# The last recurrent steps of a fused network on one Trainium2 core: state products on a 128 by 128 block diagonal, and extra products in the gaps

## What is computed

```python
h = concat(mean_over_hidden(einsum(x, W) + b), txt)     # 64 x 96 x 64
h = h + ssm_4_layers(layernorm(h))                      # state space layers
h = h + moe_top2_of_16(layernorm(h))                    # two-layer experts
h = h + attention_8_heads(layernorm(h))                 # causal, strict
h = h + lstm(layernorm(h))                              # 96 steps, one after the other

def lstm_step(h, c, x_t):                               # U_*, V_*: 64 x 64
    i = sigmoid(x_t @ U_i + b_i + h @ V_i)
    g = tanh(x_t @ U_c + b_c + h @ V_c)
    o = sigmoid(x_t @ U_o + b_o + h @ V_o)
    c = h * c + i * g
    h = o * tanh(c)
    return h, c
```

## Time and profile before

| what | value |
|---|---|
| median of 3 runs | 833.98 us (831.4 to 834.63) |
| the profiled execution's own time | 833.69 us |
| its span, first to last instruction | 832.0 us |
| first matmul of step 32, the first exposed one | 700.61 us into the span |
| share of the span in which PE is busy | 83% |
| mean granted clock of TensorE | 0.854 of full speed |

### The profile page before, as it was taken

The page is one execution under the profiler, slowest core; times in us unless marked ns, Lnnn a source line. Parts: engine busy times, 40 slices in busy tenths (PEclk is TensorE's granted clock), DMA queues, the critical chain, the costliest instruction groups (busy, mean ns, idle before and its releaser), DMA issues.

```text
span 832.0 us, 16450 instructions
## 1 busy us (share of the span) xinstructions
PE 691.6 (83%) x6414; PEld 408.9 (49%) x6414; DVE 515.8 (62%) x1098; ACT 372.8 (45%) x694; POOL 228.9 (28%) x203
## 2 busy tenths in 40 slices
PE   3677788954579999988899899989899998887775
PEld 3675545633442222245234344347577776565553
DVE  3765675568956555366458766558777774345643
ACT  2232444431424455645444455545565654333332
POOL 4156754474600032111023210214422422000000
PEclk9989789776569999999999999999899999555555
DMA  9840000000035343200232222200000000000000
GB/s 186 144 81 10 1 1 1 2 0 1 0 98 176 106 130 123 72 2 3 88 102 78 63 90 87 52 1 2 2 2 2 2 2 4 8 11 7 11 9 12
DMA packets 42402, 36.85 MB, mean 44 GB/s; under 512 B 20888, under 2 KB 29848, under 8 KB 42328
## 3 DMA queue, kind: packets, MB, share of 16 engines
q1 hardware_dynamic: 41242, 35.57, 16.4%
q10 hardware_dynamic: 1088, 0.26, 0.2%
HBM read 33.85 MB, written 1.97 MB: 43 GB/s over the span
## 4 chain that ended last, share of the span: by engine, by line
PE 55%; DVE 25%; ACT 7%; issue 6%; POOL 3%; DMA 2%; SPq 1%; DVEq 0%; POOLq 0%; ACTq 0%
PE PS L1656 10%; PE PS L1643 10%; PE PS L1619 6%; PE PS L1691 3%; PE PS L1670 3%; DVE XC L991 3%; PE PS L1605 2%; PE PS L1747 2%; PE PS L1758 2%; PE PS L1712 2%; DVE st L973 2%; DMA BIG<-in_x 2%; ACT Y L700 2%; DVE st L989 2%; DVE am L1171 2%
## 5 line engine op out<-in xcount | busy, mean ns | idle before, releaser
L1656 PE MATMUL PS<-Y,W1f 64*128 64x512 f32 x384 | 110.5, 653 | 4.8 <-DVE Y L1132 2.5
L1643 PE MATMUL PS<-XC,w2s 128*64 128x512 f32 x384 | 105.2, 627 | 0.4 <-ACT BIG L736 0.4
L1619 PE MATMUL PS<-LS,V 64*64 64x32 f32 x1140 | 70.6, 270 | 29.2 <-DVE LS L1274 29.0
L745 ACT ACTIVATE XC<-PS 128x1024 f32<-128x1024 f32 x68 | 69.3, 1021 | 53.6 <-PE PS L1643 44.9
L1619 PEld LDWEIGHTS PS<-LS,V 64*64 64x64 f32 x1140 | 58.6, 187 | 69.5 <-DVE LS L1274 66.2
L1132 DVE TENSOR_TENSOR Y<-XD,UF 128x512 f32<-128x512 f32 x96 | 67.6, 715 | 14.4 <-DMA UF<-gd 8.8
L604 POOL TENSOR_TENSOR st<-st,mhalf 128x8 f32<-128x8 f32 x12 | 21.5, 1795 | 186.5 <-DVE st L1119 186.5
L1261 DVE SCALAR_TENSOR_TENSOR LS<-LS 128x32 f32<-128x32 f32 x96 | 19.5, 203 | 63.5 <-ACT LS L860 39.9
L1643 PEld LDWEIGHTS PS<-XC,w2s 128*64 128x64 f32 x384 | 19.3, 136 | 74.2 <-issue 65.3
L1656 PEld LDWEIGHTS PS<-Y,W1f 64*128 64x128 f32 x384 | 29.9, 187 | 50.0 <-issue 25.5
L178 POOL TENSOR_TENSOR st<-st,mhalf 128x8 f32<-128x8 f32 x24 | 39.3, 1637 | 37.6 <-DVE st L976 37.6
(11 more groups left out here) (239 smaller groups left out, 1434.7 us busy)
## 6 DMA issues: line engine op xcount, KB each, us to landing
UF<-gd SPq DMA_DIRECT2D x192, 128.0 KB, 2.9
BIG<-in_x SPq DMA_DIRECT2D x8, 512.0 KB, 12.2
out<-X SPq DMA_DIRECT2D x48, 32.0 KB, 2.0
W1f<-in_L_ffn_w SPq DMA_DIRECT2D x2, 512.0 KB, 6.3
EX<-in_L_ffn_w SPq DMA_DIRECT2D x1, 1024.0 KB, 16.3
H<-in_txt SPq DMA_DIRECT2D x2, 256.0 KB, 12.5
w2s<-in_L_ffn_w SPq DMA_DIRECT2D x1, 512.0 KB, 9.2
gd<-EX SPq DMA_DIRECT2D x6, 64.0 KB, 1.7
```

Of the source, the lines that this page charges most:

```text
L745: act.activation(Hb[:, b:b + 2, :], PS[:, b:b + 2, :], ACT.Relu).then_inc(S("m_h"), 1)
L1619: mm = pe.matmul(PS[r, b, o:o + HN], V3[r, g, :], HB[r, (t - 1) % 4, :], start=False, stop=True, skip_group_check=True)
L1643: mm = pe.matmul(PS[64 * h:64 * h + 64, 6, :], w2s[:, 2 * p + h, :], Hb[:, n % 2 * 2 + h, :], start=(p == 0), stop=(p == E // 2 - 1))
L1656: mm = pe.matmul(PS[:, n % 2 * 2 + h, :], W1f[r, 2 * p + h, :], Rb[r, n % 4, :], start=True, stop=True)
```

## The change

1. A tile `VB` holds the three state matrices twice, on the diagonal of a 128 by 128 block each, with zeros elsewhere. GpSimd fills it (one memset, two copies) between the scaling of V and the subtraction on `W1f`. In the exposed steps `gates_h` makes one product per gate with weights of 128 by 128 for both halves of the batch, where there were two with 64 by 64. Steps 0 to 31 keep the pairs.
2. In every exposed step but the last, and but those with `last_project`, `att_out` or `turn_x`, PE makes one more product at the end of the slot, of `W1f` with n columns of `w2s`, whose result is read by nothing (banks 0 or 1 of PSUM, free at that time). n is 256, 448, 176 or 272 by t % 4, and 160 more in the slots where chunk 4 or 5 is normalised.
3. `last_project` moves to t = 33, 35, 37 and 39, and chunk 4 begins at t = 45 in place of 49.
4. The 24 transposes of `att_out` and `turn_x` of chunks 4 and 5 become matmuls with the identity.

```diff
+        VB = sb("VB", [128, 3, 128])
...
-        XB = (3 * E + 2, 3 * E + 13, None, None, NPR + 18, NPR + 34)
+        XB = (3 * E + 2, 3 * E + 13, None, None, NPR + 14, NPR + 34)
...
-        LAST_O = [XS + 1 + 4 * c for c in range(NP)]
+        LAST_O = [XS + 1 + 2 * c for c in range(NP)]
...
+            seq(pool.memset(VB[:, :, :], 0.0), "VB")
+            for h in range(2):
+                r = slice(64 * h, 64 * h + 64)
+                seq(pool.tensor_copy(VB[r, :, r], V3[r, :, :]), "VB")
...
+            def turn_block(c, k, src):
+
+                dst = PS[:, x_bank(c), k * 128:(k + 1) * 128]
+                if x_bank(c) == 0:
+                    return pe.matmul(dst, src, ident[:, :], start=True, stop=True)
+                return pe.transpose(dst, src, ident[:, :])
...
                     else:
+
                         b, o = (2 + gate_pair(k), (2 * s + g) * HN) if g < 2 else (6 + gate_pair(k), s * HN)
-                    for h in range(2):
+                        mm = pe.matmul(PS[:, b, o:o + HN], VB[:, g, :], HB[:, (t - 1) % 4, :], start=False, stop=True, skip_group_check=True)
+                    for h in range(2 if shared(k) else 0):
                         r = slice(64 * h, 64 * h + 64)
...
+                if g >= LS1 and t < T - 1 and t not in LAST_O and not residual(g, "ao0", "ao1", "turn"):
+
+                    n = (256, 448, 176, 272)[t % 4] + (160 if residual(g, "n0", "n1", "n2", "mu") else 0)
+                    b = 0 if t <= LAST_C[-1] + 1 else 1
+                    pe.matmul(PS[:, b, 0:n], W1f[:, 0, :], w2s[:, 0:8, :].rearrange("p e d -> p (e d)")[:, 0:n], start=True, stop=True)
```

More of the change, by code:

```diff
@@ L1571, in att_out @@
                     m = q * QM + k
-                    mm = pe.transpose(PS[:, x_bank(c), k * 128:(k + 1) * 128], AO[:, m * 128:(m + 1) * 128], ident[:, :])
+                    mm = turn_block(c, k, AO[:, m * 128:(m + 1) * 128])
                 mm.then_inc(S("ao_tp"), 1)
@@ L1578, in turn_x @@
                 for k in range(4):
-                    mm = pe.transpose(PS[:, x_bank(c), k * 128:(k + 1) * 128],
-                                      Xnrm[:, 2 * k:2 * k + 2, :].rearrange("p m d -> p (m d)"), ident[:, :])
+                    mm = turn_block(c, k, Xnrm[:, 2 * k:2 * k + 2, :].rearrange("p m d -> p (m d)"))
                 mm.then_inc(S("x_tp"), 1)
@@ L1852, in _ @@
             pe.wait_ge(S("MMs"), 2)
+            pe.wait_ge(S("VB"), 3)
             for g in range(NSLOT):
```

## The result

The change makes the kernel slower: 881.18 us median of 5 runs (879.27 to 898.76), against 833.98 (831.14 to 840.6, 5 runs) for the kernel before. The ratio is 1.0595, with a 95% interval of 1.0543 to 1.0648. Ratios in this document leave out the runs that stand more than 1.5% above the fastest of the same kernel, so they can differ a little from the quotient of the medians. The forecast was 861 us in a range of 831 to 881; the median is 0.2 us above its upper end. The profiled execution of the changed kernel took 889.54 us.

A forecast was written before the change was run, and what follows sets the result against it. TensorE heads the chain with 55%, its clock at half in the exposed steps; at half clock it would become the bound. From 833.7 us, 0.6 x 46 + 0.4 x (-3) + 1.2 = +27.6 gives 861 us, range 831 to 881.

The forecast's parts named there:

- Forecast A: Exposed steps: the clock falls and is low for a third of the stage or more, 845 to 881 us; chance 0.63.
- half clock throughout: All 60 exposed steps at half clock: +47, less 2 to 4 us, +1.2 for GpSimd, giving +45, 879 us.
- Weight loads grow with width and with the clock's period: State products: 128-wide loads 0.115 us apart at full clock, 0.22 at half; twice the width is twice the load.
- full-clock step (1.88): Exposed step with the diagonal at full clock: 1.22 + 0.67 us to the tanh = 1.88 us.
- half-clock tanh (1.11): Exposed step with the diagonal at half clock: tanh 1.11 us behind the first state product, a chain step of 2.33 us.
- C: Rival: the clock holds and wide loads keep the pair's 0.06 us pace, steps of 1.69 us, 819 us; chance 0.11.
- 2.7 us a step: Exposed steps at half clock: TensorE needs 10.7 us for four steps, against 2.33 by the chain and 1.92 now.
- The low level for 60% of the stage: Exposed steps: full clock at first and off and on later, low for 60% of the stage, weighted 0.6 x 46.
- `last_project` hidden at full clock: Its four steps: hidden in a step of 1.88 us, 2.3 us saved; at half clock about even.
- GpSimd's filling: Ahead of GpSimd's line 586: filling VB is not hidden and moves the chain, +1.2 us, bounds 0 and 1.5.
- B: Rival: the clock holds and the diagonal eats the gain, 832 us (829.5 to 836); chance 0.18.
- D: Rival: the clock toggles and comes back soon, 836 to 845 us; chance 0.08.

The follow-up runs named there:

- the third experiment: The change with 128 more columns (at most 512) in each added product; 896.13 us median of 4 runs.
- the last experiment: The change with 128 more columns per added product, stretched steps filled, 96 columns in steps 33 and 37; 842.54 us median of 11 runs in two groups.
- the seventh experiment: The change with four more products of 512 columns in each of steps 56, 72 and 88; 877.36 us, ratio 1.0433 to the kernel before.
- the first experiment: The change with state products back in pairs of 64 by 64 and no VB filling; 829.91 us, ratio 0.9952 to the kernel before.
- the fourth: The change with pairs, no VB filling and no added products, keeping the moves and identity matmuls; 836.17 us, ratio 1.0049 to the kernel before.
- the second: The kernel before with the diagonal alone, VB filled, no added products, nothing moved; 864.21 us, ratio 1.0417.
- the last two: Pairs with added products, stretched steps filled by up to 512 more columns: 821.98 us; and the diagonal with 128 more columns and such filling: 842.54 us.

## Why the prediction was right or wrong

**Mechanism and sign.** Forecast A said that the clock falls, stays low for long, and TensorE becomes the bound at half clock. The trace shows each of these, and A's own range of 845 to 881 us ends 0.2 us short of the median. What failed is the sum, in two of its terms: the length of a step at half clock, and the share of the stage at that level. The first alone puts the time past the range, whose upper end lies 2 us above "half clock throughout", +45 us for 60 steps: in the profiled execution 48 steps at half clock already cost 49.8 us. What each part costs, mean of four plain steps in us from the profiled executions:

| | full clock | half clock |
|---|---|---|
| pairs, nothing added | 1.69 (two steps) | 1.92 |
| diagonal, nothing added | 1.89 (one step) | 2.37 |
| pairs and added products | 1.71 | 2.60 |
| diagonal and added products | 1.90 | 2.91 |

**Weight loads grow with width and with the clock's period: right.** In the raw rows the starts of line 1629 are 0.112 us apart at full and 0.214 at half clock, against 0.115 and 0.22. With them the full-clock step (1.88), its tanh (0.67) and, without added products, the half-clock tanh (1.11) came out as forecast. By the Trainium skill's load time without a clock term (TensorE: Matmul & The Clock Gate, section LDWEIGHTS) the half-clock step with the diagonal alone would have been about 2.0 us, by the prediction's estimate; it was 2.37, so the rows decide against it. C, the pair's pace of 0.06 us, is out: the full-clock steps of the change decide it.

**"2.7 us a step": too small, by 0.3.** The sum was 10.7 us for four steps. The timeline of four plain steps at half clock gives 11.64:

```profile
843.98 1.33 PE L1629 MATMUL PS<-LS,VB 128*128 128x32 f32 x6
845.24 1.12 PE L1616 MATMUL PS<-XD,U 65*64 65x128 f32 x8
846.29 0.96 PE L1919 MATMUL PS<-w2s,W1f 128*128 128x176 f32 x2
...
850.00 1.33 PE L1629 MATMUL PS<-LS,VB 128*128 128x32 f32 x6
851.25 0.65 PE L1647 MATMUL PS<-ident,LS 64*32 64x64 f32 x16
851.84 1.22 PE L1919 MATMUL PS<-w2s,W1f 128*128 128x256 f32 x2
852.85 1.33 PE L1629 MATMUL PS<-LS,VB 128*128 128x32 f32 x6
853.99 1.84 PE L1919 MATMUL PS<-w2s,W1f 128*128 128x448 f32 x2
```

From start to next start, with the rows of 847.04 to 850.00 shown above: line 1629 takes 4.91 us (forecast 5.4), the added products 4.46 (4.0), `gates_x` 1.05 + 0.63 = 1.68 (1.0), `out_tp` 0.59 (0.3). The loads were sized well, even high. Two other terms were too low. I took a latency of 0.42 us off each `gates_x` and 0.31 off `out_tp`, as if what follows ran beside their ends; the next product starts only 0.06 to 0.07 us before the row's end. And I priced an added product by its columns alone: 256, 448, 176 and 272 of them are 4.03 us at 3.5 ns, and the real total is 0.4 more. That makes 2.91 us a plain step. The rest up to the 3.00 of all 48 is in the steps that carry a chunk's transposes as matmuls or 160 columns more, some of them up to 3.6 us, which the forecast had put inside the 2.7.

**"The low level for 60% of the stage": too small.** It was 48 of 63 steps, three quarters, in the profiled execution. That number was a choice, and said to be one. (The sum also took 46 us for the half-clock stage where its own line gives 45 with GpSimd's 1.2 in it, so 44; that is 1 us of the forecast.) With the forecast's own half-clock price, 46/60 = 0.77 us a step, 48 steps give 36.8 us in place of 27.6, so the share lacks 9 us; at the measured price, 49.8 / 48 = 1.04 us a step, there are 13 more. Together with -1.9 for the first 15 steps that is the 47.8 of the stage. The change, the third experiment and the last show added products that take TensorE's whole time at half clock while the clock stays low, for 149, 188 and 89 us. Just ahead of the rises in the diagonal's kernels the engine ran these at half clock: in the seventh experiment two rows of 416 columns and two of 512 (first burst), two of 416 and three of 512 (second), two of 256 and four of 512 (third); in the last experiment two of 512 and two of 384. In the change no run is longer than two rows of 448, in the third experiment none longer than two of 512. But such a run isn't the only thing that can go ahead of a rise: with pairs the clock rose behind two rows of 448 in the first experiment (750.6 us), and in the fourth, at 727 us, behind two `last_project` five microseconds apart. What decides was not isolated.

**The small parts.** `last_project` hidden at full clock: right, the first 15 steps took 1.9 us less, though two of the four steps behind it were 0.1 us over the others. GpSimd's filling was put at 1.2 us; it is about that. The timeline of the changed kernel:

```profile
68.65 0.42 POOL L581 MEMSET VB<- 128x384 f32 x1
...
69.14 0.74 POOL L584 COPY VB<-V 64x192 f32<-64x192 f32 x2
69.97 4.50 POOL L586 TENSOR_TENSOR W1f<-W1f,EX 128x2048 f32<-128x2048 f32 x1
72.69 2.33 DVE L990 TENSOR_TENSOR Y<-Y,UT 128x512 f32<-128x512 f32 x1 [3.36 <-ACT Y L700]
...
75.78 6.61 DVE L996 SCALAR_TENSOR_TENSOR XC<-st,Y 128x512 f32<-128x512 f32 x1
```

The prediction said that VectorE's line 985, now 990, would be held by GpSimd's long instruction as line 991 is: it went from 0.94 to 2.33 us and ends 0.55 us after GpSimd's line 586 does (74.47). From its start to the end of line 996 it is 9.70 us, against 8.32 before, but that stretch scatters too much for a price: it is 8.06 us in the first experiment and 10.69 in the fourth, neither of which has the filling, and 8.80 in the second, which has it. GpSimd's own rows are steadier: line 586 starts 1.38 us behind the end of the scaling of V (68.59), against 0.08 us before, so the fill adds 1.3 us there.

**The rivals.** B's price agrees with the shorter executions of the last experiment (about 833 us), and its condition isn't met by this change. C fell with the spacing of the loads, and would not have been reached with pairs either: 829.9 us and not 818, since the clock falls in the stretched steps. D, a clock that toggles and comes back by itself, isn't what the profiled execution of the change does; with the diagonal it came back only where more columns had been put in. What stays open: why the profiled executions start the exposed steps anywhere between 696.5 and 711.2 us, and what decides between the two groups of executions of the last kernel. I have only the clock rows for both. Whether the zeros in half of each diagonal block matter to the clock was not tested: no run has a block of 128 by 128 without zeros there.

## What to carry to other kernels

Work that is added to hold the clock has a price at the low clock, and that price is paid for as long as the low level lasts: put its sum at half clock beside the step first, and see that it still ends before the next input comes; here 2.3 us of chain met 2.9 us of TensorE. Put the filling into the stretches in which another engine makes the step long: with pairs that gave 1.2% here (0.6 to 1.8%), where the change's own filling gave 0.5% (0.1 to 0.9%); the intervals overlap. A longer run of dense rows at such a place can also end a low stretch, as the added bursts of the seventh experiment did; it stood ahead of the rises in the last two as well. And halving the number of small matmuls won nothing here, where their pace is that of the weight loads: a step with two 64 by 64 products per gate in different corners of the array took 1.69 us at full and 1.92 at half clock, with one of 128 by 128 on a diagonal, half of which is zeros, 1.89 and 2.37.

## What was unexpected of the hardware

- TensorE busy in 187.47 of 187.80 us with the granted clock at 0.50 the whole time: a TensorE that the profile calls busy doesn't tell which level it gets. Weight loads were in flight in 136 of these us.
- The same instruction stream ran at half clock for 89 us and then at full clock for 77 us (the last experiment), with a run of two rows of 512 and two of 384 columns between.
- With 128 by 128 transposes of 32-bit floats as the only filling the clock stayed at 1.00 for 77 us, as with products.
- A matmul of two rows with 128-wide weights at half clock holds TensorE 0.14 to 0.16 us longer than its columns (0.854 us for a row of 512, by the starts of such rows in the first burst; a product of two rows of 448 takes 1.63 us), and the change from the 128-wide state products to 64-wide tiles costs 0.12 us (1.26 us from line 1629 to `gates_x`, 1.14 to an added product). At full clock such gaps are hidden under the wait for h.
